# A new step table for a fused attention and feed-forward kernel: five steps move into the neighbouring turn, and every step and PSUM bank is placed anew

## The reference: what is computed

```
h = layernorm(x)
A: a = self_attention(h, h, h, mask_s)        # 16 heads of 16, q k v o projections with bias
   h1 = LN1(h + a)
B: a = cross_attention(h1, ctx, ctx, mask_x)  # keys and values from a second input
   h2 = LN2(h1 + a)
C: h3 = LN3(h2 + relu(h2 @ W1 + b1) @ W2)     # 256 -> 1024 -> 256
   x1 = x + tanh(g_xattn) * h3
E: y = bitlinear(silu(bitlinear(ln(x1), w_gate)) * bitlinear(ln(x1), w_up), w_down)
   out = x1 + tanh(g_ffn) * y                 # bitlinear: int8 activations, ternary weights
```

## Time and profile before

| | |
|---|---|
| median of the runs | 1058.88 us |
| the profiled execution | 1056.64 us, its span 1054.9 us |
| PE busy | 891.9 us, 85% of the span |
| DVE busy | 780.6 us, 74% |
| ACT busy | 501.2 us, 48% |
| POOL busy | 343.3 us, 33% |
| granted TensorE clock, mean | 0.954 |

### The profile page before, as it was taken

How to read it: one execution, slowest core, us unless ns; L and a number is a source line. 1 busy time by engine, 2 the same in 40 slices (tenths; PEclk the granted TensorE clock), 3 DMA queues, 4 the chain that set the end, 5 groups by cost and what they waited for, 6 DMA issues and landing times.

```text
span 1054.9 us, 25741 instructions
## 1 busy us (share of the span) xinstructions
PE 891.9 (85%) x8730; PEld 687.2 (65%) x8774; DVE 780.6 (74%) x1921; ACT 501.2 (48%) x833; POOL 343.3 (33%) x405
## 2 busy tenths in 40 slices
PE   1147678999999999999998999999999999987674
PEld 0025456767777777777786868686867777765451
DVE  7955566577878878888788888888787878666544
ACT  3123233445555646464655555555555555543433
POOL 7001313252424242424333343424242425141320
PEclk9978779999999999999999999999999999998886
DMA  5053250505050514151424232232415150302000
GB/s 173 1 154 101 70 137 22 142 22 141 23 149 24 130 41 130 41 127 37 108 59 105 60 98 73 81 85 70 101 38 132 31 130 21 77 22 66 21 11 11
DMA packets 57450, 80.81 MB, mean 77 GB/s; under 512 B 9623, under 2 KB 52798, under 8 KB 53310
## 3 DMA queue, kind: packets, MB, share of 16 engines
q1 hardware_dynamic: 57406, 80.22, 28.7%
HBM read 54.49 MB, written 25.17 MB: 76 GB/s over the span
## 4 chain that ended last, share of the span: by engine, by line
PE 49%; DVE 16%; issue 13%; POOL 11%; DMA 7%; ACT 2%; SPq 1%; POOLq 0%; DVEq 0%; ACTq 0%
PE lin_A L765 11%; PE lin_B L610 5%; PE lin_C L610 4%; PE smax L683 4%; PE lin_E L610 4%; DMA stk_BQ<-parts_BQ 3%; PE st L709 3%; PE av L723 3%; POOL lrs L1338 2%; PE lin_C L755 2%; POOL late L1402 2%; DVE late L1123 2%; POOL late L1397 2%; POOL late L1394 2%; PE lin_C L783 2%
## 5 line engine op out<-in xcount | busy, mean ns | idle before, releaser
L943 ACT ACTIVATE e<-st 128x1024 f32<-128x1024 f32 x128 | 131.1, 1025 | 83.3 <-PE st L709 82.8
L1338 POOL TENSOR_TENSOR lrs<-lve,neghalf 128x2 f32<-128x2 f32 (+1 forms) x112 | 71.0, 634 | 301.2 <-DVE lve L1118 299.9
L765 PE MATMUL lin_A<-w,late 128*128 128x256 f32 x512 | 116.8, 381 | 0.1
L1187 DVE TENSOR_REDUCE nm_A<-smax 128x4 f32<-128x512 f32 x128 | 87.9, 687 | 30.0 <-PE smax L683 28.4
L1187 DVE TENSOR_REDUCE nm_B<-smax 128x4 f32<-128x512 f32 x128 | 87.9, 686 | 25.9 <-PE smax L683 25.1
L765 PEld LDWEIGHTS lin_A<-w,late 128*128 128x128 f32 x512 | 95.8, 190 | 14.3 <-DVE late L1247 0.4
L679 PE MATMUL smax<-mb,ident_big 128*128 128x512 f16 x128 | 51.4, 401 | 33.8 <-DVE nm_A L1187 31.0
L949 ACT ACTIVATE av_sb<-av 128x512 f32<-128x512 f32 x64 | 38.2, 597 | 59.9 <-PE av L723 59.7
L683 PE MATMUL smax<-stk_BK,stk_BQ 126*128 126x128 f16 x512 | 52.0, 226 | 11.4 <-DMA stk_BQ<-parts_BQ 7.5
L1344 POOL TENSOR_TENSOR qk_AQ<-qf_A,qk_AQ 128x512 f16<-128x512 f32 x16 | 18.5, 1157 | 112.7 <-ACT qk_AQ L895 112.7
L683 PEld LDWEIGHTS smax<-stk_BK,stk_BQ 126*128 126x128 f16 x512 | 36.7, 100 | 23.8 <-DVE nm_B L1187 7.8
(11 more groups left out here) (270 smaller groups left out, 2348.8 us busy)
## 6 DMA issues: line engine op xcount, KB each, us to landing
stk_AK<-parts_AK SPq DMA_DIRECT2D x32, 256.0 KB, 3.7
stk_AQ<-parts_AQ SPq DMA_DIRECT2D x32, 256.0 KB, 3.8
stk_BK<-parts_BK SPq DMA_DIRECT2D x32, 256.0 KB, 4.5
stk_BQ<-parts_BQ SPq DMA_DIRECT2D x32, 256.0 KB, 5.0
x_a<-in_x_dram SPq DMA_DIRECT2D x16, 256.0 KB, 2.9
cx<-in_ctx_dram SPq DMA_DIRECT2D x16, 256.0 KB, 2.7
parts_AK<-qk_AK SPq DMA_DIRECT2D x16, 256.0 KB, 2.3
parts_AQ<-qk_AQ SPq DMA_DIRECT2D x16, 256.0 KB, 2.2
```

The lines of the kernel that those rows point to most:

```text
L765: mm = eng.matmul(bank[:, 0:D], fT[:, c, k * P:(k + 1) * P], w2[:, c, :], start=(c == 0), stop=(c == FC - 1))
L943: eng.activation(e32[:, hf, :], st[:, :], ACT.Exp, scale=SCORE).then_inc(st_drained, 1)
L1187: eng.tensor_reduce(nm[s][:, 4 * part:4 * part + 4], smax[:, :].rearrange("p (h k) -> p h k", h=4), AX_X, ALU.max, negate=True).then_inc(s ...
L1338: eng.tensor_tensor(lrs[n][:, a:b], lve[n][:, a:b], neghalf[:, 0:b - a], ALU.pow).then_inc(ln_rstd[n], 1)
```

## The change

A new table replaces the old one, with the same 97 steps, and a new `BANK_OF` goes with it. The old turn began at `("smax", 1, 0)`; the new one begins at `("M", 1)`. What stood ahead of it now stands at the end of the turn before. For the attention units this only needs another number (`("smax", 1, 0)` is now `("smax", 5, 0)`). The steps of `Bp` and `("E", "norm")` have no such number, so a table `SHIFT` moves five of them one turn ahead, and `of` gives each step the turn that it belongs to. `LAG` is still 4, so there are 20 turns as before, five of them written out. No instruction is added or dropped for any group; two waits for the output biases' setup (`u_bo`) move.

```diff
 SCHEDULE = [
-    ("smax", 1, 0), ("Bp", "X"), ("values", -1, 0), ("smax", 1, 1), ("values", -1, 1), ("scores", 0, 0),
...
+    ("M", 1), ("Ap", "norm"), ("N", -2), ("Bp", "Q"), ("setup", 0), ("E", "TQ"), ("values", 0, 0), ("W", -1),
...
 BANK_OF = {
-    ("B", "X"): "C", ("B", "V"): "C", ("B", ("R", -1)): "E", ("B", ("O", -1)): "C", ("E", "TQ"): "A",
...
+    ("B", "K"): "E", ("B", "T"): "E", ("B", ("R", 3)): "A", ("B", "Q"): "E", ("E", "TQ"): "A",
...
+SHIFT = {
+    ("Bp", "X"): -1, ("Bp", "K"): -1, ("Bp", "V"): -1, ("Bp", "T"): -1, ("E", "norm"): -1,
+}
...
     if step[0] in OFF:
-        return active(step[0], t)
+        return active(step[0], t - SHIFT.get(step, 0))
...
+LAG = max(last_turn_of(step) for step in SCHEDULE)
+LOOP = LAG + 1
...
+            def of(self, step):
+                return Step(self.reg, self.t - SHIFT.get(step, 0))
...
 # PE, scores(); and its start
+                    if turn.reg is None and turn.const == 0:
+                        eng.wait_ge(u_bo, 3)
...
-            iteration(first[0])
-            eng.wait_ge(u_bo, 3)
-            for st_ in first[1:3]:
+            for st_ in first[0:3]:
                 iteration(st_)
...
 # DVE
-            first = first_steps()
-            iteration(first[0])
             n_bo = [0]
             eng.wait_ge(u_pe, 8)
             setup(eng.tensor_scalar(boA[:, :], st[:, 0:D], 1.0 / WS, None, ALU.mult), u_bo, n_bo)
...
-            for st_ in first[1:]:
+            for st_ in first_steps():
                 iteration(st_)
```

More of the change, by code:

```diff
@@ L83 @@
 STAGE = {"Ap": "A", "Bp": "B", "C": "C", "E": "E"}
-LOOP = 5
 SCHEDULE = [
-    ("smax", 1, 0), ("Bp", "X"), ("values", -1, 0), ("smax", 1, 1), ("values", -1, 1), ("scores", 0, 0),
[10 rows of a table removed]
[L110 to L113, removed]
[11 rows of a table added]
+    ("scores", 3, 0), ("smax", 4, 3), ("values", 2, 1), ("E", "DN", 1, 2), ("smax", 5, 0), ("scores", 3, 1),
+    ("N", 1), ("R", 2), ("M", 4), ("smax", 5, 1), ("values", 3, 0), ("values", 3, 1), ("O", 2), ("E", "norm"),
+    ("Bp", "K"), ("smax", 5, 2), ("R", 3), ("W", 2), ("Bp", "V"), ("scores", 4, 0), ("smax", 5, 3), ("Bp", "T"),
+    ("Ap", "V"), ("O", 3), ("scores", 4, 1),
 ]
 BANK_OF = {
[8 rows of a table removed]
[8 rows of a table added]
+}
+SHIFT = {
+    ("Bp", "X"): -1, ("Bp", "K"): -1, ("Bp", "V"): -1, ("Bp", "T"): -1, ("E", "norm"): -1,
 }
@@ L146, in works @@
     if step[0] in OFF:
-        return active(step[0], t)
+        return active(step[0], t - SHIFT.get(step, 0))
     if step[0] == "in":
-        return active(step[1] + "p", t)
+        return active(step[1] + "p", t - SHIFT.get(step, 0))
     stage, _, t_unit = unit_of(t, step[1])
@@ L172, in jobs_before_setup, with last_turn_of @@
     return sum(len(jobs(bank, u)) for u in range(t)) + sum(1 for j in head if j and BANK_OF.get(j, j[0]) == bank)
+def last_turn_of(step):
+    if step[0] in OFF or step[0] == "in":
+        return OFF[step[1] + "p" if step[0] == "in" else step[0]] + SHIFT.get(step, 0)
+    return 0 if step[0] == "setup" else OFF["AB"[step[1] % 4 // 2]] - step[1] // 4
+LAG = max(last_turn_of(step) for step in SCHEDULE)
+LOOP = LAG + 1
+JOB_SHIFT = {job_of(step, t): SHIFT.get(step, 0) for step in SCHEDULE for t in range(3, LOOP + 1) if job_of(step, t)}
+PLAIN = {"A": ("T", "K"), "B": ("X", "T", "Q"), "C": ("T",), "E": ()}
 def highs(stage, t):
-    plain = {"A": ("T", "K"), "B": ("X", "T", "Q"), "C": ("T",)}[stage]
     found = [job_of(step, t) for step in SCHEDULE]
-    return [j for j in found if j and j[0] == stage and j[1] in plain]
+    return [j for j in found if j and j[0] == stage and j[1] in PLAIN[stage]]
 def head_at(slot):
@@ L389, in __init__ @@
                 self.g = {s: Turn(reg, t - OFF[s]) for s in OFF}
+            def of(self, step):
+                return Step(self.reg, self.t - SHIFT.get(step, 0))
             def count(self, which, where, job, back=0):
-                now = which(where, self.t - back)
+                turn = self.t - back + JOB_SHIFT[job]
+                now = which(where, turn)
                 if job not in now:
@@ L397, in count @@
                     return 0
-                over = sum(len(which(where, t)) for t in range(self.t - back)) + now.index(job) + 1
+                over = sum(len(which(where, t)) for t in range(turn)) + now.index(job) + 1
                 return over if self.reg is None else self.reg * len(now) + over
@@ L439, in last_steps @@
         def last_steps(first=NG):
-            return [Step(None, t) for t in range(first, NG + OFF["E"])]
+            return [Step(None, t) for t in range(first, NG + LAG)]
         PART_OUT = {"Q": 32, "K": 16}
@@ L511, in parts_in, with iteration @@
                                   rows).then_inc(stk_in[s, t], 16)
-            def iteration(st_, more_x=True):
-                g = st_.g
+            def iteration(turn):
                 for step in SCHEDULE:
-                    if not works(step, st_.t):
+                    if not works(step, turn.t):
                         continue
+                    st_ = turn.of(step)
+                    g = st_.g
                     if step[0] == "in":
@@ L562, in _ @@
             for st_ in last_steps(NG - 1):
-                iteration(st_, more_x=False)
+                iteration(st_)
             eng.wait_ge(out_done, 16 * NB)
@@ L784, in beside, with iteration @@
                 mm.then_inc(fill, 1)
-            def iteration(st_):
+            def iteration(turn):
                 for step in SCHEDULE:
-                    if not works(step, st_.t):
+                    if not works(step, turn.t):
                         continue
+                    st_ = turn.of(step)
                     what, name = step[0:2]
@@ L1158, in prep @@
                 whole = lambda t: t[:, :, :].rearrange("p c n -> p (c n)")
-                if s in "ABC" and (s, name) in highs(s, st_.t):
+                if name in PLAIN[s]:
                     eng.wait_ge(high[s], st_.high_value(s, name))
```

2 lines of the change are left out of this document (1 added, 1 removed), and 34 rows, old and new, of tables (BANK_OF, SCHEDULE).

## The result

The changed kernel takes 1045.67 us (median of four runs, 1044.83 to 1047.82) against 1058.84 us before (1058.14 to 1060.01): a ratio of 0.988, 95% interval 0.986 to 0.989. The profiled execution took 1044.83 us, its span 1042.5 us. The forecast was 1047, range 1033 to 1066. The sum came out, within 2 us; several of its terms didn't.

The account below looks back on a forecast made before the run. TensorE was taken to bound the middle, 95.4% busy. Thirteen turns saving 1.4 us each (-18), the start +6 and the end 0 gave -12 on 1056.64, 1044.6; with 2.2 for the runs' median, 1047 us, range 1033 to 1066.

Parts of the forecast that it names:

- What bounds, and the stall: Middle: TensorE 95.4% busy; its idle mostly smax waiting for VectorE's reduction, 1.8 us a turn, largest 1.43 behind nrm_B.
- The VectorE chain, 21.4 us: Turn's first part, F2's end to B's Q: VectorE's queue ends it at 21.4 us against TensorE's 21.0, gaining 1.4.
- the meetings with GpSimd: First part of the turn: VectorE instructions held by simultaneous GpSimd ones, 1.1 us taken as already in the 21.4.
- the second part: The turn from B's Q to the end of the second F2: 31.97 us plus a new 0.35 wait, 32.3.
- the slower rival: First part: GpSimd holds VectorE in three meetings, 3.8 us; chain 24.1, turn 56.4, whole 1082 us; chance 0.21.
- the 22.3 from which it decides: First-part VectorE chain length, 0.9 over the forecast's, from which the turns save less than the start costs.
- The wait for B's Q through DRAM, 0.35 us: Second part: nrm_B ahead of B's low half delays Q's DRAM round before B's first smax; 0.35 us, bounds 0 and 0.6.
- PE full: Middle: queues interlock better, neither VectorE's 0.4 nor B's Q wait shows; 2.1 us a turn saved, 1035 us; chance 0.12.
- The stall only moves: First part: the 1.4 us wait returns at reductions between E's norm and M; time stays at 1059; chance 0.11.
- The start, 6 us: Before the steady turns: later first norm and weight work make first smax late; costs 6 us, bounds 3 and 8.
- The end, 0 give or take 2: Draining turns: same steps of C and E in the same order, costed at 0, give or take 2 us.

Follow-up runs that it names:

- kernel 1: The kernel before (old table) with only the normalisation of B's first item moved into the next turn, behind the first norm: 1053.15 us, ratio 0.993.
- kernel 6: The changed kernel with all its work, but GpSimd starts hres_A only after VectorE's second part of the split of the maxima: 1032.27 us, ratio 0.974.
- kernel 9: kernel 6 with LN3's bias addition waiting for the first split, nrm_A behind R, and turn 0's setup laid out anew: 1022.87 us, ratio 0.965.
- kernels 1 to 3: Old table: kernel 1, kernel 2, and the kernel before with GpSimd's hres_A waiting for the end of nrm_B of B's first item (1054.33 us, ratio 0.995).
- kernels 4 to 7: kernel 4; the changed kernel with hres_A on one column after turn 0 (1034.54 us); kernel 6; kernel 6 with LN3's addition and nrm_A also delayed (1027.68 us).
- 8 and 9: The changed kernel with only turn 0's output-bias and weight setup placed later (1042.79 us, ratio 0.984); and kernel 9.
- kernel 2: The kernel before with only the normalisation of B's first item moved into the next turn, ahead of the first norm: 1053.99 us, ratio 0.995.
- kernel 4: The changed kernel with the normalisation of B's first item put back behind its statistics: 1052.35 us, ratio 0.993 to the kernel before.

## Why the prediction was right, and where not

**What bounds, and the stall.** Right. The wait for `nm_A` went wholly, and moving the normalisation is worth the 1.4 us in its own part (31.10 against 32.50 in kernel 1). That this comes from the one move is only half the matter: in the old table the part after it gives 1.2 back, and the new table with the normalisation put back already has a turn of 54.62 instead of 55.2. The gain of the middle lies in the table as a whole.

**The VectorE chain, 21.4 us.** This step failed, and the term that was too small is the meetings with GpSimd: they were taken at 1.1 us and measured about 2.5. The part came to 22.4 us. The other terms that I summed are there (the norm's wait is 0.9, W's statistics and `nrm_A` come in). The part is 1.0 longer than forecast and not 1.4; one reason is that three small waits for TensorE (0.16, 0.22 and 0.17 us before), which my sum had kept, are gone, against one new one of 0.28. With all three taken apart the turn is 52.90; less the 31.96 of the second part that leaves 20.9, below my 21.4 and at TensorE's own 21.0. The middle gained 0.75 a turn and not 1.4: at 54.36 us it lies just outside the 53.2 to 54.3 that I had called the forecast, and the sign that I had given for the slower rival, splits of over 1 us with TensorE waiting behind them, is there in every turn. The slower rival had the right mechanism, place by place; it was too dear, since `nrm_A` was held for half of its partner only, and the chain stopped at 22.4, on the edge of the 22.3 from which it decides, with a second part 0.3 shorter than forecast.

The Trainium skill ("SBUF — State Buffer", Who interferes with whom) says which VectorE instructions contend with GpSimd: those in a two-port mode, which `tensor_scalar` can enter, and those with two inputs in SBUF beside a GpSimd instruction that reads SBUF; outside these modes one with at most one input in SBUF does not, nor does a reduction. The trace agrees on each: L1222 and L1151 held, L1224 held, the low half L1192 at 0.69 beside `hres_A` (kernel 6). Applied instruction by instruction to the new order it would have named all three as ones that can be held; I used it for the rival's price and not for my own sum.

**The wait for B's Q through DRAM, 0.35 us.** Wrong: it is 0. The second part is 31.96 us, of which 31.96 busy, where I had 32.3. `nrm_B` does make the low half of Q 0.3 us later, as I had it. What failed is that TensorE's work between Q and that smax "stays within 0.1 us": from one to the other are 13.36 us (455.92 to 469.28) where there were 12.94 (455.32 to 468.26), and the 0.4 cover the delay.

**PE full.** As a path for this change it didn't come. As a bound it did: kernel 9 stands there.

**The stall only moves.** Right in the main for kernels 1 to 3 in the old table, and partly here: three waits of 1.3 us together in place of 2.1 (1.8 for `nm_A` at smax and 0.25 at M).

**The start, 6 us.** The working holds to the first smax (81 to 82 forecast, 81.17 measured). The step that failed is that all but 2 us of it would last. The first F2 scatters: 204.7 to 209.5 in five kernels with the old start, 206.8 to 209.3 in five with the changed one (after and kernels 4 to 7), 206.0 and 204.0 with the new start of 8 and 9. The means are 206.9, 208.2 and 205.0. The means of the first two differ by 1.4 us, and kernels with the same start by up to 4.8, so what the change's start costs is known only as some 0 to 3 us, less than the 6 forecast. Why turns 1 and 2 give the rest back wasn't tried.

**The end, 0 give or take 2.** Wrong, 7.6 us in three intervals, of which 3 x 0.75 = 2.2 belongs to the turn. Kernel 1 alone gains 6.0 there and kernel 2 7.3, and kernel 4 keeps 5.3 with the normalisation put back, so either the move or the rest of the table shortens these turns, and the two don't add up. I had counted by work. TensorE's work in them did not change and its idle time fell by 7.1 us, so waits between the stages set their length; which of them each move shortens was not tested.

So the errors cancelled, and that the sum came out is luck: with thirteen turns, the start and the end as forecast -18, +6 and 0, together -12; measured in the profiled executions -8.1 for twelve intervals, +2.9 for the start, -7.6 for the drain and +0.4 for what follows it, together -12.4.

## What to carry to other kernels

When an order of steps changes, list for each engine pair which instructions now run at the same time, and price each meeting of GpSimd with a VectorE instruction of the kinds that were held here at the rest of GpSimd's instruction; here one added wait on GpSimd, which makes it start some 0.6 us later, was worth as much as the whole new table. Look again after each shift: in two of the runs the later GpSimd instruction met another VectorE instruction. Moving one step out of a critical stretch is only worth what the stretch that takes it can cover, on every engine that the step uses. Don't sum the draining turns by work: here TensorE idled 25 of their 147 us.

## What the runs showed of the hardware

Held by a GpSimd `tensor_tensor` that had started first were these VectorE instructions, all with their operands in SBUF: `tensor_scalar` and `scalar_tensor_tensor` on 128 x 16 values, 0.17 us alone and 1.12 to 1.21 in the middle of the changed kernel, beside one of 1.26 or 1.27 (0.65 and 0.75 before, where less of GpSimd's was left); `tensor_scalar` on 128 x 2, 0.17 alone and 0.93 (kernel 4); the normalisation on 128 x 256, 0.41 alone and 0.98 or 1.28. The narrow ones ended 0.03 us after GpSimd's, the normalisation 0.15. Not held: reductions from PSUM (0.67 to 0.69 us everywhere), the low halves, one input of which is in PSUM (0.67 to 0.69), and `bn_stats` from SBUF (a pair took 0.74 to 0.75).

In the three meetings GpSimd's own instruction was not longer for it (1.26 to 1.28 us). It had started first there. Where VectorE had started first, GpSimd was held. In the start of the changed kernel, VectorE, then GpSimd:

```profile
70.63 1.22 DVE L1115 TENSOR_SCALAR late<-late 128x2048 f32<-128x2048 f32 x1
71.88 2.06 DVE L1116 TENSOR_SCALAR late<-late 128x2048 bf16<-128x2048 f32 x1
```

```profile
71.46 1.40 POOL L1371 TENSOR_TENSOR qk_AQ<-qf_A,qk_AQ 128x512 f16<-128x512 f32 x1 [15.07 <-ACT qk_AQ L922]
72.82 2.24 POOL L1411 TENSOR_TENSOR hres_A<-h,boA 128x512 f32<-128x512 f32 x1
```

Alone, L1116 takes 1.23 us, `qk_AQ` 1.16 and `hres_A` 1.27. `hres_A` ends 1.1 us after VectorE's instruction, nearly its whole length.
